# A four-layer graph network on one core: the last layer's unit loop written out, its destination keys copied by ScalarE, its sums spread over four PSUM banks

## The chip, the cores and the metric

The kernel runs on one core of a Trainium2 chip. The metric is the device time of one execution in microseconds (us). Before the change the median of three runs is 14387.95 us (14383.14 to 14405.51).

## The reference, cut to what matters

There are 12500 nodes with 64 features each and 400000 edges, sorted by destination. Four layers follow one another; each normalises x, clips it at zero and adds a graph operation to x. The change lies in the last layer:

```
message   = h[dst] * edge_weight[:, None]
neigh_agg = segment_sum(message, src, num_segments=12500)
x = x + (h @ W_self.T + b_self + neigh_agg @ W_neigh.T + b_neigh)
```

The edges are sorted by `dst`, but this layer sums over `src`, so its messages have to be brought into another order first.

## The kernel before, in words

A node is numbered by its lane (one of 128 partitions, called q here) and its place in the lane (one of 98, r). The last layer works in two parts.

The first part (`body4`, 125 blocks of 25 edges per lane) makes a record of 98 words for each edge: three bf16 planes of the message, whose sum is the fp32 message, and in the last two words the q of the node it belongs to. GpSimd scatters the records by indirect DMA (L1180) into `records` in DRAM, so that all records of one r lie together in groups of 512 (`SG`). There is room for 880 groups (`GMAX`).

The second part, which the change touches, walks over the 880 groups in 220 units (`UNITS`) of 4 groups (`UG`), 16 columns (`UC`) of 128 records each. For unit u:

- SyncE waits until unit u-4 has been summed (semaphore `unit_summed`), then loads the unit's 2048 records (784 KB) into one of four buffers `rows4[u % 4]` (L1095; semaphore `rows_in0` to `rows_in3`).
- VectorE copies each record's q twice into `qtwice[u % 2]` (bf16, L1671), and compares it with an iota row: this gives 16 one-hot matrices of 128 x 128 in `ohs4[u % 2]` (helper `row_onehots`, whose instruction is on L686; semaphore `unit_onehot`). It first waits for `unit_summed` of unit u-2, which frees that buffer.
- TensorE multiplies one-hots and message planes: 16 columns x 3 planes = 48 matmuls with 64 moving columns (L1971) into one PSUM bank, `bk[u % 2]`, 64 columns of the bank for each group. Before that it waits for `unit_running` of unit u-2, which frees the bank.
- VectorE adds the groups up in a chain (`unit_running`): running sum = previous running sum * mask + sum of this group, four instructions (L1684). The mask (`keepg`, one column per group) is zero where a new r begins. The four masks of a unit are first copied to `keep4` (L1675), as the column's number is in a register.
- ScalarE waits for `unit_running` and stores the four running sums (128 KB) to `by_lane`, a view of the DRAM tensor `sums` (L1825; semaphores `running_out0`, `running_out1`). The two `running` buffers alternate.

VectorE's order of work is written out: one-hots of u, running sums of u-1, one-hots of u+1, and so on. The helper `units` (L968) makes units 0 to 3 with numbers known at compile time, and the rest in a hardware loop of four units a turn, where waits compare with registers. `wait` issues a wait; `gate` issues a semaphore increment between two waits. `loop_chain` gives each VectorE instruction an increment of `v_loop` and a wait for it right behind; `clear` resets it.

When all 220 units are stored, the rows that end each r are fetched from `by_lane` (`fetch` on SyncE and ScalarE, L1188 on GpSimd), and the last matrix product and the output follow.

Of the kernel before, what the change touches and what calls it, by code (L numbers as in the profile page):

```python
# [14 lines left out]
N, E, D = 12500, 400000, 64  # L15
P = 128
# [5 lines left out]
BLOCKS = LANE // K  # L22
# [24 lines left out]
UG = 4  # L47
UNITS = GMAX // UG
RW = 98
# [8 lines left out]
def build(nc, x, src, dst, edge_weight, l0_w1, l0_b1, l0_w2, l0_b2, l1_w, l1_b,  # L58
          l2_w1, l2_b1, l2_w2, l2_b2, l3_ws, l3_bs, l3_wn, l3_bn, out):
    f32, bf16, i32, u8 = mybir.dt.float32, mybir.dt.bfloat16, mybir.dt.int32, mybir.dt.uint8  # L60
    ALU, ACT, AX = mybir.AluOpType, mybir.ActivationFunctionType, mybir.AxisListType
# [4 lines left out]
    with ctx:  # L66
        def sb(name, shape, dt=f32):
            return ctx.enter_context(nc.sbuf_tensor(name, shape, dt))

        def ps(name, shape):  # L70
            return ctx.enter_context(nc.psum_tensor(name, shape, f32))
# [3 lines left out]
        def sem(name):  # L75

            if name not in sems:
                sems[name] = ctx.enter_context(nc.semaphore(name))
            return sems[name]
# [23 lines left out]
        by_lane = sums.rearrange("(p g) f -> p g f", p=P)  # L103
# [20 lines left out]
        mblk = sb("mblk", [P, 2, K])  # L124
        rtwice = sb("rtwice", [P, K, 2], bf16)
        inrank, atbase = sb("inrank", [P, K]), sb("atbase", [P, K])
        keep4 = sb("keep4", [P, UG])
        ident_b = sb("ident_b", [P, P], bf16)
        laneg_i = sb("laneg_i", [P, 1], i32)
        endg_i = sb("endg_i", [P, TILES], i32)  # L130
# [55 lines left out]
        zero_row = sb("zero_row", [P, D])  # L186
# [13 lines left out]
        om = [ps(f"om{k}", [P, 512]) for k in range(2)]  # L200
# [5 lines left out]
        bk = [ps(f"bk{k}", [P, 512]) for k in range(2)]  # L206
# [9 lines left out]
        def mm_banks(name, u):  # L216
# [50 lines left out]
        keepg = flat(crow[:, :, :])[:, 0:GMAX]  # L267
        UC = UG * SUB_ROWS
        rows4 = [RF[:, k * UC * RW:(k + 1) * UC * RW].rearrange("p (c f) -> p c f", f=RW) for k in range(4)]
        planes4 = [[RF[:, k * UC * RW:(k + 1) * UC * RW].bitcast(bf16).rearrange("p (c f) -> p c f", f=2 * RW)  # L270
                    [:, :, a * D:(a + 1) * D] for a in range(3)] for k in range(4)]
        ohs4 = [RF[:, 4 * UC * RW + k * UC * P // 2:4 * UC * RW + (k + 1) * UC * P // 2].bitcast(bf16)
                .rearrange("p (c q) -> p c q", q=P) for k in range(2)]
        qtwice = [sb(f"qtwice{k}", [P, UC, 2], bf16) for k in range(2)]
        run_at = 4 * UC * RW + UC * P
        running = [RF[:, run_at + k * UG * D:run_at + (k + 1) * UG * D].rearrange("p (g f) -> p g f", f=D)
                   for k in range(2)]
# [19 lines left out]
        def wait(e, name, n):  # L297

            if not (isinstance(n, int) and n <= 0):
                e.wait_ge(sem(name), n)  # L300

        def gate(e):

            e.sem_inc(sem("gate_" + e.engine.name), 1)  # L304
# [378 lines left out]
        def row_onehots(e, to, twice, m):  # L683

            n = twice.shape[1]
            return e.tensor_tensor(to[:, 0:n, :].rearrange("p k (q h) -> p k q h", h=2),  # L686
                                   iota_b[:, 0:m].rearrange("p (q h) -> p q h", h=2).unsqueeze(1)
                                   .broadcast_to([P, n, m // 2, 2]),
                                   twice.unsqueeze(2).broadcast_to([P, n, m // 2, 2]), ALU.is_equal)
# [263 lines left out]
        NF = len(FILLQ)  # L953
        fill_banks = (tp[0], tp[1], om[0])
        msg_banks = (om[1], bk[0], bk[1], mixed)
        assert K == 8 * len(fill_banks) + 1


        def fetch(e, mine):

            e.wait_ge(sem("cleared"), 2)
            for k in range(2):
                e.wait_ge(sem(f"running_out{k}"), 16 * UNITS // 2 + 16 * (1 - k))
            for t in mine:
                g = e.value_load(endg_i[0:1, t:t + 1], min_val=0, max_val=GMAX)  # L965
                e.dma_start(M[:, t:t + 1, :], by_lane[:, bass.ds(g, 1), :]).then_inc(sem(f"rows_in{t // (4 * NT)}"), 16)  # L966

        def units(e, body):  # L968

            for k in range(4):  # L970
                body(k, k)
            with e.Fori(1, UNITS // 4) as j:  # L972
                for k in range(4):
                    body(j * 4 + k, k)
# [219 lines left out]
        def _(e):  # L1194
# [22 lines left out]
            def take_ab(p, t, n):  # L1217
# [7 lines left out]
                                         in1=dst_f[:, 0:LANE - 1], op0=ALU.add, op1=ALU.is_lt,  # L1225
# [6 lines left out]
            with unsorted(e):  # L1232
# [3 lines left out]
            loop_chain = Chain(e, "v_loop")  # L1236
# [9 lines left out]
                                         op0=ALU.add, op1=ALU.add))  # L1246
# [42 lines left out]
            for ins in divide_steps(e, src_v, LANE, src_q, src_r, src_i, src_i.bitcast(i32)):  # L1289
                chain(ins)  # L1290
            chain(e.scalar_tensor_tensor(out=src_v, in0=dst_f[:, :], scalar=float(P), in1=src_q,
                                         op0=ALU.mult, op1=ALU.add))
# [370 lines left out]
            e.sem_inc(sem("cleared"), 1)  # L1663


            def unit_onehots(u, k):
                wait(e, f"rows_in{k}", (u - k) * 4 + 16)
                gate(e)
                wait(e, "unit_summed", u - 1)
                gate(e)  # L1670
                loop_chain(e.tensor_copy(qtwice[k % 2][:, :, :], rows4[k][:, :, RW - 2:RW - 1].broadcast_to([P, UC, 2])))  # L1671
                row_onehots(e, ohs4[k % 2], qtwice[k % 2][:, :, :], P).then_inc(sem("unit_onehot"), 1)

            def unit_running(u, k):
                loop_chain(e.tensor_copy(keep4[:, :], keepg[:, bass.ds(u * UG, UG)]))  # L1675
                wait(e, "unit_summed", u + 1)
                gate(e)
                wait(e, f"running_out{k % 2}", (u - k % 2) * 8 + 16 * (1 - k % 2))
                gate(e)
                for g in range(UG):  # L1680
                    prev = running[k % 2][:, g - 1, :] if g else running[1 - k % 2][:, UG - 1, :]
                    if isinstance(u, int) and u + g == 0:
                        prev = zero_row[:, :]
                    loop_chain(e.scalar_tensor_tensor(out=running[k % 2][:, g, :], in0=prev, scalar=keep4[:, g:g + 1],  # L1684
                                                      in1=bk[k % 2][:, g * D:(g + 1) * D], op0=ALU.mult, op1=ALU.add))
                loop_chain.clear()
                e.sem_inc(sem("unit_running"), 1)

            def unit(u, k):
                unit_onehots(u, k)  # L1690
                if not (isinstance(u, int) and u == 0):
                    unit_running(u - 1, (k - 1) % 4)
            units(e, unit)
            unit_running(UNITS - 1, 3)
            for g in range(NGROUPS + 1):
                if g < NGROUPS:
                    mine = len([t for t in range(g // 2 * 2 * NT, (g // 2 + 1) * 2 * NT) if t % 3 == 0])
# [10 lines left out]
        def _(e):  # L1708
# [110 lines left out]
                            .then_inc(sem("middles"), 1)  # L1819
            loop(e, body4)  # L1820

            def unit(u, k):
                wait(e, "unit_running", u + 1)
                gate(e)
                e.dma_start(by_lane[:, bass.ds(u * UG, UG), :], running[k % 2])\  # L1825
                    .then_inc(sem(f"running_out{k % 2}"), 16)
            units(e, unit)
            fetch(e, range(2, TILES, 3))
            for g in range(NGROUPS):
                mm_scalar(e, "last", g)  # L1830
# [3 lines left out]
        def _(e):  # L1834
            e.wait_ge(sem("const"), 1)
            e.wait_ge(sem("checked"), 1)
            for c in range(2):
                last = e.matmul(pb[0:1, 0:1], bad[:, c:c + 1], ones[:, 0:1], start=c == 0, stop=c == 1)
# [9 lines left out]
            for g in range(NGROUPS // 2):  # L1848
                e.wait_ge(sem("rows_vector"), g + 1)
                for k in range(2 * NT):  # L1850
                    last = e.matmul(pa[:, :], mark_u[:, k // 2, :, k % 2], mark_v[:, k // 2, :, k % 2], start=g + k == 0,
                                    stop=g == NGROUPS // 2 - 1 and k == 2 * NT - 1, skip_group_check=True)
# [82 lines left out]
            for a in range(2):  # L1935
                last = e.transpose(pa[:, a * D:(a + 1) * D], w_lastT[:, a, :], ident[0:D, 0:D])
# [26 lines left out]
            def unit(u, k):  # L1963
                wait(e, "unit_onehot", u + 1)
                gate(e)
                wait(e, "unit_running", u - 1)
                gate(e)
                for c in range(UC):
                    g, part = c // SUB_ROWS, c % SUB_ROWS
                    for a in range(3):  # L1970
                        last = e.matmul(bk[k % 2][:, g * D:(g + 1) * D], ohs4[k % 2][:, c, :], planes4[k][a][:, c, :],  # L1971
                                        start=part + a == 0, stop=part == SUB_ROWS - 1 and a == 2)
                last.then_inc(sem("unit_summed"), 1)
            units(e, unit)
            mm_tensor(e, "last", D, "aggregated", 3 * NGROUPS)

# [22 lines left out]
```

## Time and profile before

| | us |
|---|---|
| median of 3 runs | 14387.95 |
| lowest, highest | 14383.14, 14405.51 |
| profiled execution, time | 14387.05 |
| profiled execution, span | 14385.3 |
| VectorE busy | 9170.4 (64% of the span) |
| GpSimd busy | 7813.4 (54%) |
| TensorE matmul busy | 7309.5 (51%) |
| ScalarE busy | 5834.6 (41%) |
| DMA, mean over the span | 137 GB/s |

The span is the time from the first to the last instruction in the trace. Busy times are sums over stages with different limits, so the rows read below are those of the second part of the last layer, from 13450 us to 14264 us of the span. The page calls the engines PE (TensorE), DVE (VectorE), ACT (ScalarE), POOL (GpSimd) and SP (SyncE); a q behind the name means the engine's sequencer or its DMA queue. The granted clock of TensorE is given as a share of its full speed: 1.00 is 2.4 GHz, 0.50 is 1.2 GHz.

### The profile page before, as it was taken

Reading aid. Unit: us, or ns where it says so; the run is one execution under the profiler, and the core shown is the slowest. Engines: PE = TensorE matmul, PEld = TensorE weight load, DVE = VectorE, ACT = ScalarE, POOL = GpSimd, SP = SyncE. Lnnn points to the kernel's source line nnn. Section 1 sums busy time; section 2 is a strip of 40 time slices with the busy share of each in tenths; the row PEclk is TensorE's granted clock in tenths of the full one; section 3 lists DMA queues with packets and bytes.
Section 4 is the critical chain, followed back from the end, with each engine's and each line's share of the span. In section 5 each row is a group of like instructions: output and inputs, shape, how many; then the busy total and the mean of one; then the engine's idle time right before and its main releaser. Section 6 shows DMA issues by size and latency. Waiting matters only on the chain. (4 is left out here: it accounts for less than half of the span.)

```text
span 14385.3 us, 285255 instructions
## 1 busy us (share of the span) xinstructions
PE 7309.5 (51%) x96792; PEld 5290.3 (37%) x96792; DVE 9170.4 (64%) x18447; ACT 5834.6 (41%) x10200; POOL 7813.4 (54%) x7194
## 2 busy tenths in 40 slices
PE   2266666666666646996999799600000000000355
PEld 1255555555555533553555555400000000000355
DVE  5488888888888884335333333466666666666575
ACT  0144444444444434774677477432222222222000
POOL 5677777777777751110111011377777777777300
PEclk9866666666666668997999899755555555555676
DMA  7333333333333328664866766322222222221585
GB/s 313 125 115 115 113 117 110 116 111 118 109 118 109 118 86 287 196 196 161 270 197 186 268 195 196 117 67 65 67 62 65 65 64 65 64 65 60 170 255 181
DMA packets 1267102, 1969.49 MB, mean 137 GB/s; under 512 B 255577, under 2 KB 986558, under 8 KB 1261425
## 3 DMA queue, kind: packets, MB, share of 16 engines
q1 hardware_dynamic: 861601, 1047.59, 24.0%
q10 hardware_dynamic: 172928, 612.08, 10.8%
q0 software_dynamic: 231664, 297.80, 7.7%
q8 instruction: 558, 9.14, 0.3%
q14 instruction: 351, 2.88, 0.1%
HBM read 1155.02 MB, written 815.55 MB: 137 GB/s over the span
## 5 line engine op out<-in xcount | busy, mean ns | idle before, releaser
L633 POOL DMA_INDIRECT RF<-tab_edge_b,idx x3125 | 3549.9, 1136 | 1029.5 <-issue 947.5
L1180 POOL DMA_INDIRECT records<-RF,idx x3125 | 3141.8, 1005 | 984.5 <-issue 984.5
L686 DVE TENSOR_TENSOR HM<-iota_b,eqw 128x2048 bf16<-128x2048 bf16 x2000 | 2204.3, 1102 | 344.8 <-PE bk L1865 198.0
L1739 ACT ACTIVATE X<-bk 128x392 uint8<-128x392 f32 x4000 | 1783.3, 495 | 1564.3 <-PE bk L1865 1546.1
L877 POOL DMA_INDIRECT agg<-RF,lastT x372 | 520.6, 1399 | 3209.9 <-ACT RF L819 3119.1
L1865 PE MATMUL bk<-HM 128*64 128x98 bf16 x32000 | 1581.3, 247 | 1310.0 <-ACT X L1739 661.2
L1865 PE MATMUL kp<-HM,ident_b 128*64 128x98 bf16 x6250 | 281.5, 283 | 3793.5 <-DVEq L1642 3793.5
L777 PE MATMUL tp<-HM,RF 128*64 128x512 bf16 x12276 | 2117.6, 383 | 91.0 <-ACT HM L729 66.3
L1865 PEld LDWEIGHTS bk<-HM 128*64 128x64 bf16 x32000 | 1237.2, 134 | 1657.4 <-issue 1575.6
L1865 PEld LDWEIGHTS kp<-HM,ident_b 128*64 128x64 bf16 x6250 | 261.5, 168 | 3814.5 <-issue 3814.5
L783 PE MATMUL om<-HM,RF 128*64 128x512 bf16 x6138 | 1422.2, 382 | 0.0
L777 PE MATMUL tp<-RF 128*64 128x512 bf16 x5952 | 1099.3, 388 | 262.8 <-ACT RF L729 236.9
L777 PEld LDWEIGHTS tp<-HM,RF 128*64 128x64 bf16 x12276 | 923.6, 110 | 727.7 <-issue 178.9
L1393 DVE SCALAR_TENSOR_TENSOR RF<-RF,dupjunk 128x64 f32<-128x64 f32 x3124 | 870.4, 279 | 27.3
L1393 DVE SCALAR_TENSOR_TENSOR RF<-RF,dupjunk,om 128x64 f32<-128x64 f32 x3124 | 848.5, 272 | 0.4
L1804 ACT ACTIVATE RF<-qblk 128x50 f32<-128x50 f32 x125 | 31.7, 254 | 1993.6 <-DMA records<-RF,idx 1940.7
L729 ACT ACTIVATE RF<-dst_f 128x4096 bf16<-128x4096 uint8 x186 | 672.8, 3617 | 354.7 <-PE tp L777 235.2
L729 ACT ACTIVATE HM<-dst_f 128x4096 bf16<-128x4096 uint8 (+1 forms) x186 | 703.5, 3823 | 138.2 <-DMA dst_f<-counts 89.9
L731 DVE CAST HM<-dst_f 128x4096 bf16<-128x4096 uint8 x186 | 426.9, 2295 | 500.9 <-PE tp L777 204.3
L783 PE MATMUL om<-RF 128*64 128x512 bf16 x2976 | 742.0, 388 | 0.0
L729 ACT ACTIVATE HM<-crow 128x4096 bf16<-128x4096 uint8 x186 | 671.6, 3611 | 54.2 <-DMA crow<-counts 40.6
L777 PEld LDWEIGHTS tp<-RF 128*64 128x64 bf16 x5952 | 496.2, 112 | 535.4 <-issue 299.4
(364 smaller groups left out, 15242.4 us busy)
## 6 DMA issues: line engine op xcount, KB each, us to landing
dst_f<-counts SPq DMA_DIRECT2D x465, 512.0 KB, 3.8
RF<-first_rows SPq DMA_DIRECT2D x250, 800.0 KB
counts<-X ACTq DMA_DIRECT2D x250, 784.0 KB
RF<-records SPq DMA_DIRECT2D x220, 784.0 KB
crow<-counts SPq DMA_DIRECT2D x279, 512.0 KB, 3.8
records<-RF ACTq DMA_DIRECT2D x2, 57680.0 KB, 214.4
first_rows<-RF ACTq DMA_DIRECT2D x25, 4000.0 KB, 49.4
edge_rows<-RF ACTq DMA_DIRECT2D x125, 800.0 KB
```

The costliest lines, as they stand in the source:

```text
L633: e.indirect_dma_start(out=ring[:, r, j, :], out_offset=None, in_=table[:, :], in_offset=bass.IndirectOffsetOnAxis(ap=idx[:, r, j:j + 1], ...
L686: return e.tensor_tensor(to[:, 0:n, :].rearrange("p k (q h) -> p k q h", h=2), iota_b[:, 0:m].rearrange("p (q h) -> p q h", h=2).unsqueeze ...
L729: e.activation(to, of, ACT.Copy).then_inc(sem("widened_A"), 1)
L731: e.tensor_copy(to, of).then_inc(sem("widened_D"), 1)
L777: last = e.matmul(tp[u][k * D:(k + 1) * D, :], hi_mid[:, t, k * D:(k + 1) * D], part, start=t == 0, stop=t == TILES - 1, skip_group_check= ...
L783: return e.matmul(om[u][k * D:(k + 1) * D, :], low[:, t, :], part, start=t < 2, stop=t >= TILES - 2, skip_group_check=True)
L877: e.indirect_dma_start(out=agg[:, :], out_offset=bass.IndirectOffsetOnAxis(ap=lastT[:, g * GB + k:g * GB + k + 1], axis=0), in_=out_rows[g ...
L1180: e.indirect_dma_start(out=records[:, :], out_offset=bass.IndirectOffsetOnAxis(ap=idx2[:, r, j:j + 1], axis=0), in_=msgs[MSG_OF[r]][:, j, ...
L1393: e.scalar_tensor_tensor(out=buf[:, r, j, :], in0=prev, scalar=mask[:, j:j + 1], in1=this, op0=op0, op1=op1).then_inc(sem(chain.name), 1)
L1739: e.activation(staged[u].rearrange("p (r k) -> p r k", k=P)[:, :, k:k + 4], bk[s % 2][:, 0:4 * TILES].rearrange("p (k r) -> p r k", k=4), ...
L1804: e.activation(msgs[MSG_OF[r]][:, :, RW - 2:RW], qblk[:, r, :].unsqueeze(2).broadcast_to([P, K, 2]), ACT.Copy)
L1865: last = e.matmul(to[k:k + D, :], by_q[:, k:k + D], by_r, start=start, stop=stop, skip_group_check=True)
```

## The change

ScalarE makes the copies of q, two units ahead of the stores (`unit_keys`), and signals them with `keyed`, a semaphore that stands at 125 (`BLOCKS`) by then. VectorE reads the masks in `keepg` directly, and its part and ScalarE's are unrolled in Python for all 220 units with constant numbers, with plain waits and no gates. The sums go to four PSUM banks in turn (`unit_banks`), and TensorE waits for `unit_running` of unit u-4 instead of u-2. SyncE and TensorE stay in the hardware loop.

```diff
--- before.py
+++ after.py
@@ -124,7 +124,6 @@
         mblk = sb("mblk", [P, 2, K])
         rtwice = sb("rtwice", [P, K, 2], bf16)
         inrank, atbase = sb("inrank", [P, K]), sb("atbase", [P, K])
-        keep4 = sb("keep4", [P, UG])
         ident_b = sb("ident_b", [P, P], bf16)
         laneg_i = sb("laneg_i", [P, 1], i32)
         endg_i = sb("endg_i", [P, TILES], i32)
@@ -953,6 +952,7 @@
         NF = len(FILLQ)
         fill_banks = (tp[0], tp[1], om[0])
         msg_banks = (om[1], bk[0], bk[1], mixed)
+        unit_banks = (bk[0], bk[1], om[0], om[1])
         assert K == 8 * len(fill_banks) + 1
 
 
@@ -1663,35 +1663,29 @@
             e.sem_inc(sem("cleared"), 1)
 
 
-            def unit_onehots(u, k):
-                wait(e, f"rows_in{k}", (u - k) * 4 + 16)
-                gate(e)
+            def unit_onehots(u):
+                e.wait_ge(sem("keyed"), BLOCKS + u + 1)
                 wait(e, "unit_summed", u - 1)
-                gate(e)
-                loop_chain(e.tensor_copy(qtwice[k % 2][:, :, :], rows4[k][:, :, RW - 2:RW - 1].broadcast_to([P, UC, 2])))
-                row_onehots(e, ohs4[k % 2], qtwice[k % 2][:, :, :], P).then_inc(sem("unit_onehot"), 1)
-
-            def unit_running(u, k):
-                loop_chain(e.tensor_copy(keep4[:, :], keepg[:, bass.ds(u * UG, UG)]))
-                wait(e, "unit_summed", u + 1)
-                gate(e)
-                wait(e, f"running_out{k % 2}", (u - k % 2) * 8 + 16 * (1 - k % 2))
-                gate(e)
+                row_onehots(e, ohs4[u % 2], qtwice[u % 2][:, :, :], P).then_inc(sem("unit_onehot"), 1)
+
+            def unit_running(u):
+                e.wait_ge(sem("unit_summed"), u + 1)
+                wait(e, f"running_out{u % 2}", (u - u % 2) * 8 + 16 * (1 - u % 2))
                 for g in range(UG):
-                    prev = running[k % 2][:, g - 1, :] if g else running[1 - k % 2][:, UG - 1, :]
-                    if isinstance(u, int) and u + g == 0:
-                        prev = zero_row[:, :]
-                    loop_chain(e.scalar_tensor_tensor(out=running[k % 2][:, g, :], in0=prev, scalar=keep4[:, g:g + 1],
-                                                      in1=bk[k % 2][:, g * D:(g + 1) * D], op0=ALU.mult, op1=ALU.add))
-                loop_chain.clear()
-                e.sem_inc(sem("unit_running"), 1)
-
-            def unit(u, k):
-                unit_onehots(u, k)
-                if not (isinstance(u, int) and u == 0):
-                    unit_running(u - 1, (k - 1) % 4)
-            units(e, unit)
-            unit_running(UNITS - 1, 3)
+                    prev = running[u % 2][:, g - 1, :] if g else running[1 - u % 2][:, UG - 1, :] if u else zero_row[:, :]
+                    if g:
+                        e.wait_ge(sem("v_loop"), u * (UG - 1) + g)
+                    else:
+                        wait(e, "unit_running", u)
+                    e.scalar_tensor_tensor(out=running[u % 2][:, g, :], in0=prev, scalar=keepg[:, u * UG + g:u * UG + g + 1],
+                                           in1=unit_banks[u % 4][:, g * D:(g + 1) * D], op0=ALU.mult, op1=ALU.add)\
+                        .then_inc(sem("v_loop" if g < UG - 1 else "unit_running"), 1)
+
+            for u in range(UNITS + 1):
+                if u < UNITS:
+                    unit_onehots(u)
+                if u:
+                    unit_running(u - 1)
             for g in range(NGROUPS + 1):
                 if g < NGROUPS:
                     mine = len([t for t in range(g // 2 * 2 * NT, (g // 2 + 1) * 2 * NT) if t % 3 == 0])
@@ -1819,12 +1813,21 @@
                             .then_inc(sem("middles"), 1)
             loop(e, body4)
 
-            def unit(u, k):
-                wait(e, "unit_running", u + 1)
-                gate(e)
-                e.dma_start(by_lane[:, bass.ds(u * UG, UG), :], running[k % 2])\
-                    .then_inc(sem(f"running_out{k % 2}"), 16)
-            units(e, unit)
+
+            def unit_keys(u):
+                k = u % 4
+                e.wait_ge(sem(f"rows_in{k}"), u // 4 * 16 + 16)
+                wait(e, "unit_onehot", u - 1)
+                e.activation(qtwice[u % 2][:, :, :], rows4[k][:, :, RW - 2:RW - 1].broadcast_to([P, UC, 2]), ACT.Copy)\
+                    .then_inc(sem("keyed"), 1)
+
+            unit_keys(0)
+            unit_keys(1)
+            for u in range(UNITS):
+                if u + 2 < UNITS:
+                    unit_keys(u + 2)
+                e.wait_ge(sem("unit_running"), u + 1)
+                e.dma_start(by_lane[:, u * UG:(u + 1) * UG, :], running[u % 2]).then_inc(sem(f"running_out{u % 2}"), 16)
             fetch(e, range(2, TILES, 3))
             for g in range(NGROUPS):
                 mm_scalar(e, "last", g)
@@ -1963,12 +1966,12 @@
             def unit(u, k):
                 wait(e, "unit_onehot", u + 1)
                 gate(e)
-                wait(e, "unit_running", u - 1)
+                wait(e, "unit_running", u - 3)
                 gate(e)
                 for c in range(UC):
                     g, part = c // SUB_ROWS, c % SUB_ROWS
                     for a in range(3):
-                        last = e.matmul(bk[k % 2][:, g * D:(g + 1) * D], ohs4[k % 2][:, c, :], planes4[k][a][:, c, :],
+                        last = e.matmul(unit_banks[k][:, g * D:(g + 1) * D], ohs4[k % 2][:, c, :], planes4[k][a][:, c, :],
                                         start=part + a == 0, stop=part == SUB_ROWS - 1 and a == 2)
                 last.then_inc(sem("unit_summed"), 1)
             units(e, unit)
```

## Rows read from the trace of the kernel before

**Rows 1.** The page's 40 slices: busy tenths of VectorE, granted clock tenths.
```profile
DVE  5488888888888884335333333466666666666575
...
PEclk9866666666666668997999899755555555555676
```

**Rows 2.** The page's chain that ended last, by line.
```profile
POOL records L1180 22%; DVE RF L1684 1%; PE bk L1971 1%; DVE RF L686 1%; PE om L383 0%; DVE qtwice L1671 0%; DVE keep L1675 0%; PE tp L370 0%; DVEq L304 0%; ACTq L965 0%; DVEq L300 0%; ACTq L966 0%; PE bk L370 0%; POOL first_rows L920 0%; DVEq L972 0%
```

**Rows 3.** A window of 250 us: us, busy time (instructions) by engine, clock, DMA.
```profile
13700.00:13950.00 250.00, 140.28 (x3279) 132.62 (x3275) 177.83 (x478) 0.00 (x0) 0.00 (x0) 0.78 0.81 255
```

**Rows 4.** Timeline over some units: start, us, instruction [idle before, releaser].
```profile
13702.33 1.59 PE L1971 MATMUL bk<-RF 128*128 128x64 bf16 x48 [1.90 <-DVE RF L686]
...
13704.63 0.18 DVE L1671 CAST qtwice<-RF 128x32 bf16<-128x32 f32 x1 [0.85 <-PE bk L1971]
13704.84 1.23 DVE L686 TENSOR_TENSOR RF<-iota_b,qtwice 128x2048 bf16<-128x2048 bf16 x1
13705.99 0.16 DVE L1675 COPY keep<-crow 128x4 f32 x1
...
13706.53 1.23 DVE L1684 SCALAR_TENSOR_TENSOR RF<-RF,keep,bk 128x64 f32<-128x64 f32 x4 [0.38 <-DVE keep L1675]
13708.16 0.18 DVE L1671 CAST qtwice<-RF 128x32 bf16<-128x32 f32 x1 [0.40 <-DVE RF L1684]
...
13709.90 2.72 PE L1971 MATMUL bk<-RF 128*128 128x64 bf16 x48 [1.58 <-DVE RF L686]
...
13719.29 0.18 DVE L1671 CAST qtwice<-RF 128x32 bf16<-128x32 f32 x1 [0.85 <-DVE RF L1684]
```

**Rows 5.** Groups by line and shape, 13500 to 14250 us: busy, mean, idle.
```profile
L1971 PE MATMUL bk<-RF 128*128 128x64 bf16 x9826 | 418.5, 212 | 333.0 <-DVE RF L686 333.0
...
L686 DVE TENSOR_TENSOR RF<-iota_b,qtwice 128x2048 bf16<-128x2048 bf16 x205 | 251.3, 1226 | 7.1
L1684 DVE SCALAR_TENSOR_TENSOR RF<-RF,keep,bk 128x64 f32<-128x64 f32 x819 | 230.0, 281 | 103.7 <-DVE keep L1675 81.8
L1671 DVE CAST qtwice<-RF 128x32 bf16<-128x32 f32 x204 | 37.0, 182 | 105.0 <-PE bk L1971 60.1 <-DVE RF L1684 44.9
L1675 DVE COPY keep<-crow 128x4 f32 x205 | 33.5, 163 | 0.0
```

**Rows 6.** Timeline of the first units of the second part.
```profile
13451.47 23.71 SPq L1095 DMA_DIRECT2D RF<-records  x9
13456.14 0.18 DVE L1671 CAST qtwice<-RF 128x32 bf16<-128x32 f32 x1 [84.67 <-DMA RF<-records]
...
13457.88 4.75 PE L1971 MATMUL bk<-RF 128*128 128x64 bf16 x96 [91.35 <-DVE RF L686]
```

**Rows 7.** One window while the first four loads land.
```profile
13454.00:13461.00 7.00, 3.12 (x59) 3.15 (x60) 3.04 (x6) 0.00 (x0) 0.00 (x0) 0.50 1.06 390
```

**Rows 8.** DMA queues, 13500 to 14250 us: packets, MB, share.
```profile
q1 hardware_dynamic: 108119, 164.43, 70.3%
q10 hardware_dynamic: 29436, 26.80, 11.1%
```

**Rows 9.** The store's line L1825 in the whole trace: durations ns, and landing.
```profile
L1825 ACTq DMA_DIRECT2D sums<-RF x220: 338/344/410, 13462.3 to 14264.1; - x110
...
DMA to landing us min/median/max: 1.7/2.1/4.8
```

**Rows 10.** Windows of 10 us with the two clock levels.
```profile
13520.00:13530.00 10.00, 7.43 (x134) 7.01 (x131) 7.17 (x19) 0.00 (x0) 0.00 (x0) 0.50 0.87 274
13540.00:13550.00 10.00, 4.59 (x143) 4.43 (x144) 7.11 (x20) 0.00 (x0) 0.00 (x0) 1.00 0.83 249
```

**Rows 11.** ScalarE's copy of q in the first part, L1804.
```profile
L1804 ACT ACTIVATE RF<-qblk x125: 248/250/273, 9332.0 to 13354.8; 128x50 f32<-128x50 f32 x125
```

**Rows 12.** Timeline behind the last unit: what GpSimd waited for.
```profile
14266.63 0.98 POOL L1188 DMA_INDIRECT HM<-sums,end_i  x1 [816.62 <-DMA sums<-RF]
```

**Rows 13.** The page's DMA queues: the instruction packets.
```profile
q8 instruction: 558, 9.14, 0.3%
```


## The prediction

> **What bounds the kernel now.** I read the page's slices first. The second part of the last layer lies in slices 38 and 39 of them, and VectorE is only 6 or 7 tenths busy there, while TensorE's granted clock is about 7 tenths [rows 1]; no engine is full on the face of it. The page's chain of what ended last then says where the part sits: behind GpSimd's scatter (L1180) with 22% come the part's own lines, L1684, L1971, L686, L1671 and L1675 [rows 2]. So the part is on the path. It begins at 13456 us with the first copy of q [rows 6], and GpSimd's fetch at 14266.63 us, which waited 816.62 us for stores to `sums`, shows that nothing behind it starts before the last store [rows 12]. A microsecond won in a unit is won 220 times.
>
> A window in its middle gives VectorE 177.83 us of 250 us, DMA a share of 0.81 at 255 GB/s and matmuls 140.28 us [rows 3]. The timeline shows what the 250 us are made of. The reader is to compare the copy of q at 13704.63 us with the one at 13719.29 us: both have the long gap of 0.85 us ahead of them, that of the loop's turn, and they are four units apart, so a unit takes 14.66 / 4 = 3.66 us [rows 4]. The groups agree: 205 units in 750 us, 3.66 us each [rows 5]. Within a unit VectorE goes without a break except for waits of its own making: copy of q 0.18, one-hots 1.23, mask copy 0.16, a gap of 0.38, four sums 1.23, a gap of 0.40 [rows 4]. The gaps stay as long when the matmuls last 1.59 us as when they last 2.72 us, and TensorE idles 333.0 us in 750 us waiting for one-hots (L686) [rows 4, 5]. VectorE with its semaphore steps is the bound, not TensorE and not the loads: 220 x 3.66 = 805 us.
>
> **The change part by part.**
>
> *VectorE.* Gone are the copy of q (37.0 us / 204 = 0.18 us), the mask copy (33.5 / 205 = 0.16 us, of which 0.08 us lies over the end of the one-hots, 13704.84 + 1.23 - 13705.99) [rows 4, 5], the gates, the clear with its increment, and the loop's turn, 0.85 - 0.40 = 0.45 us in four units or 0.11 us a unit [rows 4]. What stays is 1.23 + 1.23 = 2.46 us, the latter with the waits between the sums in it: 4 x 0.281 is 1.12, so a satisfied wait on the engine's own last result costs (1.23 - 1.12) / 3 = 0.035 us [rows 4, 5]. Left between them are three waits ahead of the sums and two ahead of the one-hots. From below they cost nothing (they pass while the engine still works, as the mask copy began before the one-hots ended); from above, the gap of 0.40 us holds six semaphore steps, 0.07 us each, so five cost 0.35 us [rows 4]. I take 0.14, nearer to the wait of 0.035 us, since the reset and the increments that drained the engine are gone. VectorE then needs 2.60 us a unit, bounds 2.46 and 2.81. The masks read in place cost nothing: a scalar operand of the same kind, another address.
>
> *What is late next.* Four candidates stand close together.
>
> Loads and stores: a unit moves 784 KB in and 128 KB out, 0.934 MB. While the first four loads landed, the queues moved 390 GB/s [rows 7]; at that rate a unit takes 2.39 us, the lower bound. In the steady state the share was 0.81 of 3.66 us, which is 2.97 us if a packet takes as long when the queues are full [rows 3]; that is the upper bound. The queues' rows say the same: 70.3% + 11.1% of 750 us over 204 units is 2.99 us [rows 8]. The share in the first window is 1.06 at 390 GB/s, so packets get faster when the queue is full (368 GB/s at a share of one, against 255 / 0.81 = 315); I take 2.65 us, nearer to that window. The Trainium skill ("DMA: Bandwidth & Descriptors", Where 436 GB/s comes from) puts HBM's limit for one core at about 358 GB/s; by it a unit would be 0.934 / 358 = 2.61 us, an estimate. This trace shows more for these very loads, 390 GB/s, so the row goes before the page here.
>
> Matmuls: 1.59 us at the full clock and 2.72 us at half [rows 4, 10]. With two one-hot buffers a unit's ring over two periods is: sums 1.23, one-hots 1.23, TensorE's start behind them (copy of q at 13708.16, 0.21 us to the one-hots as in the unit before, 1.23 us of them, so 13709.60; matmuls at 13709.90: 0.30 us), matmuls, and an assumed 0.1 us back to VectorE. At half clock 1.23 + 1.23 + 0.30 + 2.72 + 0.1 = 5.58, or 2.79 us a unit; with the waits I take 2.85. At full clock it is 4.45 / 2 = 2.22 us, no bound. The two units in the first rows run 96 matmuls in 4.75 us without a break, so TensorE's own loop adds nothing that I can see [rows 6]. The four banks take the wait for the sums of u-2 away; the one-hot buffers still tie unit u to the matmuls of u-2, so the banks alone buy little, and I give them 0 (they cannot cost either: same matmuls, other addresses).
>
> ScalarE: a copy of q, 0.25 us for a similar one [rows 11], and the store's issue of 0.34 us [rows 9], 0.6 us of 2.7. It has been idle here but for the issues. What queues behind its waits: the store of u stands behind the copy of q for u+2, and that behind `rows_in` of u+2; the copy for u+3 stands behind the store of u, hence behind the sums of u. VectorE wants that copy only after one-hots u+2 and sums u+1, 2.5 us later, which covers 0.34 + 0.25 and the semaphores. At the stage's start the detour costs about 0.3 us once.
>
> Stores: `running[u % 2]` is free when the store of u has landed. Two periods must hold sums 1.23, ScalarE's hop 0.2, landing 2.1 (median) to 4.8 (longest) [rows 9]: 3.5 to 6.2 us, so 1.8 to 3.1 us a unit. The median is no bound. Loads: the first copy of q came 4.67 us behind the first load's issue [rows 6]; a load is issued when u-4 is summed, some 2.5 periods before it is wanted, so it has 6.5 us.
>
> *Sum.* At full clock max(2.60, 2.65, 2.22) = 2.65 us, at half clock 2.85 us. The clock was 0.78 in the middle, which is 0.56 of the time at 1.00 and 0.44 at 0.50, as the windows show it flip between the two [rows 3, 10]. I keep that mix: 0.56 x 2.65 + 0.44 x 2.85 = 2.74 us. 220 x 2.74 = 603 us against 805, 202 us less. The profiled execution took 14387.05 us, 0.9 us less than the median of the runs, so the sum may be taken from the median: 14388 - 202 = 14186 us. Bounds of the unit, 2.50 to 3.10 us, give 14133 to 14265 us.
>
> **Rivals.**
>
> *The transfers bound at their steady price.* If a packet keeps its length of the steady state, a unit needs 2.97 us: 14388 - 220 x 0.69 = 14236 us. For it: the share of 0.81 is that of many packets, the 390 GB/s of a few; stores lie between the loads there. Against: the share of 1.06 at a higher rate.
>
> *The clock stays up.* Matmuls would fill 1.59 of 2.6 us instead of 1.59 of 3.66, and the gaps between bursts shrink from 2.1 to 1.0 us. If TensorE is then granted 1.00 throughout and waits hide under work, a unit takes 2.50 us: 14388 - 255 = 14133 us. For it: it was 1.00 in stretches with matmuls busy only 4.6 of 10 us, and their share will rise [rows 10]. Against: it was 0.50 in stretches with matmuls busy 7.4 of 10 us [rows 10]. The Trainium skill ("TensorE: Matmul & The Clock Gate", HAM oscillation) says likewise that idle gaps throw the clock back and short ones keep it; the trace shows the flip itself, not what gap it takes.
>
> *The store waits in ScalarE's queue.* Stores behind `rows_in` of u+2 land late and each takes the longest landing, 4.8 us [rows 9], plus 0.3 for the copy: 2T = 1.23 + 0.2 + 0.34 + 0.3 + 4.8, T = 3.4 us, and 14331 us. For it: stores share the engines with loads that are now back to back. Against: a median of 2.1 us at a share of 0.81.
>
> *Slower: code that starves.* VectorE and ScalarE now run straight through code for 220 units instead of turning in a loop, and that code comes by DMA, past queues that the loads fill: the page has 558 instruction packets of 9.14 MB in all, 16.4 KB each [rows 13]. If an engine stood still for a late packet for the longest landing seen, 4.8 us [rows 9], the 202 us won are gone after 42 such stops; at one stop in every four units, 55 of them, it is 14186 + 264 = 14450 us. Against: the packets took 0.3% of the engines over the whole span, and five or ten instructions a unit is little code. The Trainium skill ("Runtime: NRT & Kernel Launch", Instruction fetch mechanics) says that a block holds 256 instructions and is fetched ahead, and that straight code hides it; by it some 2600 instructions on VectorE are 10 blocks, 48 us by the price above if none were hidden, an estimate.
>
> *It does nothing,* because something the trace doesn't name sets 3.66 us: 14388 us. The gaps' regularity speaks against it.
>
> **How the numbers follow.** The forecast 0.50 (its own range 14150 to 14225), transfers 0.22, clock up 0.13, stores late 0.08, starving code 0.05, nothing 0.02. Within 0.2% (29 us) is about what a measurement of this kernel can't tell from no change. Faster is 0.50 + 0.22 + 0.13 + 0.08 = 0.93, same 0.02, slower 0.05. The range of 8 in 10 takes in the first three cases: 14115 (2.42 us a unit, the transfers' lower bound rounded) to 14275 us (3.15).
>
> **What would show it.** Copies of q and L1675 gone from VectorE, and a period of 2.6 to 2.9 us; one-hots that begin right behind the sums, or 0.1 us later. If the waits ahead of the one-hots end with `keyed` and the DMA share is near 1, the transfers bound; if the sums wait for L1971 in stretches of clock 0.50 only, the matmuls' ring does; if they wait for nothing but stores have landings over 4 us, the `running` buffers do. The time from the last store to the end should stay about 121 us. The forecast is wrong if the period is above 3.1 us, or if VectorE shows stops that no semaphore explains.

## The result and the profile after

The changed kernel took 14163.34 us (median of 4 executions, 14156.65 to 14175.62) against 14385.55 us for the kernel before (14375.16 to 14405.51, 4 executions): ratio 0.9846, 95% interval 0.9832 to 0.986, so 222 us or 1.5% faster. The forecast was 14186 us, 202 us faster.

The page of the changed kernel answers to [rows 1]: VectorE's tenths and the granted clock.

```profile
DVE  5388888888888885335333433366656666656585
...
PEclk9866666666666667998999799955555555555598
```

The last two clock digits were 7 and 6 and are 9 and 8. The windows of the second part, 250 us and 500 us long, answer to [rows 3] (us, busy time and instructions of PE, PEld, DVE, ACT, POOL, clock, DMA share, GB/s):

```profile
13700.00:13950.00 250.00, 155.66 (x4530) 146.78 (x4531) 211.19 (x472) 21.84 (x94) 0.00 (x0) 0.97 1.02 353
13500.00:14000.00 500.00, 308.27 (x8896) 290.71 (x8892) 416.00 (x928) 43.22 (x186) 0.00 (x0) 0.97 1.01 347
```

VectorE went from 177.83 to 211.19 us busy in 250 us, the DMA share from 0.81 to 1.02, the clock from 0.78 to 0.97. How long the part takes is read from what GpSimd's first fetch waited for, as in [rows 12], where it was 816.62 us:

```profile
14055.10 0.98 POOL L1188 DMA_INDIRECT HM<-sums,end_i  x1 [609.33 <-DMA sums<-RF]
```

816.6 - 609.3 = 207.3 us are the part's own. The profiled spans differ by 14385.3 - 14173.9 = 211.4 us; the rest lies ahead of the part, whose first load is issued 4.2 us earlier, at 13447.24 instead of 13451.47 us. From the fetch to the end it is 118.7 us before and 118.8 us after. A unit takes 609.3 / 220 = 2.77 us if the start and the end of the part are shared out over the units, and 500 / 186 = 2.69 us in its middle, by the groups that answer to [rows 5]:

```profile
L685 DVE TENSOR_TENSOR RF<-iota_b,qtwice 128x2048 bf16<-128x2048 bf16 x186 | 226.6, 1218 | 0.3
...
L1680 DVE SCALAR_TENSOR_TENSOR RF<-RF,crow,bk 128x64 f32<-128x64 f32 x372 | 104.3, 280 | 39.5 <-DMA sums<-RF 27.0 <-PE bk L1974 0.7 <-issue 0.4
L1680 DVE SCALAR_TENSOR_TENSOR RF<-RF,crow,om 128x64 f32<-128x64 f32 x370 | 103.7, 280 | 44.2 <-DMA sums<-RF 33.1
L1821 ACT ACTIVATE qtwice<-RF 128x32 bf16<-128x32 f32 x186 | 43.2, 232 | 457.3 <-DMA RF<-records 378.2 <-DVE RF L1680 66.2 <-DVE RF L685 12.9
```

Both copies are gone from VectorE, and nothing is idle ahead of the one-hots (0.3 us in 500). Ahead of the sums 39.5 + 44.2 = 83.7 us are idle, and 27.0 + 33.1 = 60.1 us of them are put down to the store, `DMA sums<-RF`; for most of the rest the view names nothing. The timeline, to be read beside [rows 4], shows both kinds of unit:

```profile
13708.28 1.23 DVE L1680 SCALAR_TENSOR_TENSOR RF<-RF,crow,bk 128x64 f32<-128x64 f32 x4
...
13709.42 1.22 DVE L685 TENSOR_TENSOR RF<-iota_b,qtwice 128x2048 bf16<-128x2048 bf16 x1
13709.54 0.34 ACTq L1830 DMA_DIRECT2D sums<-RF  x1
...
13710.66 1.23 DVE L1680 SCALAR_TENSOR_TENSOR RF<-RF,crow,bk 128x64 f32<-128x64 f32 x4
...
13711.06 1.60 PE L1974 MATMUL om<-RF 128*128 128x64 bf16 x48 [0.79 <-DVE RF L685]
...
13711.92 0.34 ACTq L1830 DMA_DIRECT2D sums<-RF  x1
...
13715.84 0.23 ACT L1821 ACTIVATE qtwice<-RF 128x32 bf16<-128x32 f32 x1 [3.07 <-DMA RF<-records]
13716.27 1.23 DVE L1680 SCALAR_TENSOR_TENSOR RF<-RF,crow,om 128x64 f32<-128x64 f32 x4 [0.93 <-DMA sums<-RF]
13717.42 1.22 DVE L685 TENSOR_TENSOR RF<-iota_b,qtwice 128x2048 bf16<-128x2048 bf16 x1
```

From the sums at 13708.28 to those at 13710.66 us is 2.38 us: sums and one-hots follow each other with no gap to speak of. The one-hots start 0.09 us ahead of the end of the sums, the sums 0.02 us behind the end of the one-hots. The sums at 13716.27 us waited 0.93 us for a store. Their buffer's earlier store had been issued at 13711.92 us; they start 4.35 us later. Stores now land later than in [rows 9] (2.1 us median, 4.8 at most):

```profile
DMA to landing us min/median/max: 1.7/3.8/6.1
```

The timelines also show what a store lands with. SyncE issues the load of unit u+2 once TensorE is through with u-2, a little ahead of the store of u-2. Here is that load for the store at 13711.92 us, and the landing of all loads:

```profile
13710.54 0.37 SPq L1095 DMA_DIRECT2D RF<-records  x1
```

```profile
DMA to landing us min/median/max: 4.3/5.3/9.1
```

The load had landed when ScalarE's copy of q, which waited for it, started at 13715.84 us, 5.30 us after its issue; the store, issued 1.38 us behind it, landed by 13716.27 us, 0.43 us behind the load. In 126 of the 217 units behind the first three the sums start 0.4 us after such a copy. In run4 below, where the sums wait for no store, none do. So the store's landing seems to be set by the load issued just ahead of it. That is read from the timelines; no run changed the order of the two, so it isn't shown.

### The profile page after: what moved, and what is told of

It reads as the page before. It is cut to its first block and busy times, and to the rows that moved or that the text cites. A ratio compares the mean times of both kernels' runs of the same rounds, so it can differ in the third digit from the quotient of the medians.

```text
span 14173.9 us, 282965 instructions
## 1 busy us (share of the span) xinstructions
PE 7230.5 (51%) x96792; PEld 5213.9 (37%) x96792; DVE 9087.6 (64%) x18007; ACT 5880.2 (41%) x10420; POOL 7807.9 (55%) x7194
```

## The experiments

The part's length is GpSimd's wait for `DMA sums<-RF`; divided by 220 it is the length of a unit with the part's start and end in it. It is taken from one profiled execution of each kernel. Kernels with the same time of the kernel before beside them ran together, on one chip.

| kernel | time, us (median) | before beside it | part, us | per unit, us |
|---|---|---|---|---|
| before | 14385.55 | | 816.6 | 3.71 |
| changed | 14163.34 | 14385.55 | 609.3 | 2.77 |
| run4 | 14121.49 | 14383.55 | 554.4 | 2.52 |
| half_loads | 14080.76 | 14383.55 | 514.8 | 2.34 |
| banks_only | 14382.86 | 14383.55 | 815.8 | 3.71 |
| two_banks | 14143.63 | 14383.55 | 577.6 | 2.63 |
| after_again | 14173.28 | 14381.69 | 609.0 | 2.77 |
| unrolled_only | 14181.9 | 14381.69 | 612.8 | 2.79 |
| written_out | 14152.92 | 14381.69 | 596.0 | 2.71 |
| run4_two_banks | 14115.21 | 14381.69 | 553.4 | 2.52 |
| after_third | 18822.64 | 19051.63 | 592.2 | 2.69 |
| two_banks_again | 18818.31 | 19051.63 | 592.0 | 2.69 |
| vector_keys | 18795.44 | 19051.63 | 575.2 | 2.61 |
| keys_run4 | 18794.6 | 19051.63 | 564.5 | 2.57 |

The last four ran together on a chip where the kernel before takes 19052 us instead of 14384; the second part of the last layer has about its usual length there, other stages don't. They are compared with one another only, and by the length of the part.

**run4: four buffers of running sums.**

```diff
-                   for k in range(2)]
+                   for k in range(4)]
...
+        out_sems = (("running_out0", 16), ("running_out1", 0), ("lane_placed", 32), ("records_zeroed", 48))
...
-                wait(e, f"running_out{u % 2}", (u - u % 2) * 8 + 16 * (1 - u % 2))
+                e.wait_ge(sem(out_sems[u % 4][0]), u // 4 * 16 + out_sems[u % 4][1])
...
-                    prev = running[u % 2][:, g - 1, :] if g else running[1 - u % 2][:, UG - 1, :] if u else zero_row[:, :]
+                    prev = running[u % 4][:, g - 1, :] if g else running[(u - 1) % 4][:, UG - 1, :] if u else zero_row[:, :]
```

(`running[u % 4]` in the sums and the store too, and the fetches wait for all four semaphores.)

> The changed kernel with four buffers for the running sums instead of two; everything else as changed. After the change a unit takes 2.69 us, VectorE's own work 2.37 us. Theory A, the ring of the two buffers for running sums: a store lands 3.7 us (median) behind its issue, and the sums of u+2 wait for it. With four buffers that wait goes, and a unit falls to 2.40 to 2.50 us: 45 to 60 us less than the changed kernel (14163), about 14110. Theory B, the transfers' rate: the queues are full (share 1.00 at 347 GB/s) and the late stores are only where that shows. The unit stays at 2.65 to 2.70 us, the time within 10 us of 14163, and the wait moves to the copy of q, so to the loads.

Measured: 14121.49 us (14112.16 to 14130.0), ratio to before 0.9819 (0.9803 to 0.9835). The end of the part, and VectorE's and ScalarE's longest waits in it (us in total, times, longest):

```profile
13995.87 0.98 POOL L1189 DMA_INDIRECT HM<-sums,end_i  x1 [554.43 <-DMA sums<-RF]
```

```profile
DVE RF L685 <- ACT qtwice L1822: 27.1, 64, 1.3
DVE RF L1681 <- PE bk L1975: 1.1, 2, 0.9
```

```profile
ACT qtwice L1822 <- DMA RF<-records: 476.4, 213, 3.5
```

VectorE no longer waits for a store, though stores land later still:

```profile
DMA to landing us min/median/max: 1.7/4.7/6.2
```

Theory A holds: the two `running` buffers were the changed kernel's bound. The time is 42 us less than the changed kernel's, where 45 to 60 were forecast. In the window below VectorE runs 510 instructions, five a unit, so 102 units; a unit takes 250 / 102 = 2.45 us, where the changed kernel has 2.69, and that is inside the 2.40 to 2.50 forecast. The next bound stands right behind it: 27.1 us now go to one-hots that wait for copies of q, and 213 of the 220 copies wait for their load.

```profile
13500.00:13750.00 250.00, 162.53 (x4895) 153.07 (x4896) 225.81 (x510) 23.72 (x102) 0.00 (x0) 1.00 1.05 381
```

The queues run at 381 GB/s. That is the 0.934 MB of a unit over its 2.45 us, so it is no second proof; what speaks for the loads as the bound here are the waits. So Theory B named the second limit, not the first.

**half_loads: half of each load.** The kernel leaves out two of the four groups of records in every load; all other work stays.

```diff
-                e.dma_start(rows4[k].rearrange("p (g c) f -> p g (c f)", c=SUB_ROWS),
+                e.dma_start(rows4[k].rearrange("p (g c) f -> p g (c f)", c=SUB_ROWS)[:, 0:2, :],
...
-                            .rearrange("(g p c) f -> p g (c f)", g=UG, p=P)).then_inc(sem(f"rows_in{k}"), 16)
+                            .rearrange("(g p c) f -> p g (c f)", g=UG, p=P)[:, 0:2, :]).then_inc(sem(f"rows_in{k}"), 16)
```

> The changed kernel, but each load brings only two of the unit's four groups of records; the other half of the buffer keeps what it held, so the sums of those groups are left wrong. 0.52 MB move per unit instead of 0.93. Theory B (transfers' rate): a unit falls to VectorE's own 2.37 us plus little, 2.40, and the time to about 14100; stores land after 2.1 us again. Theory A (the ring of buffers, a fixed landing): also faster only if landings shorten, so landings stay near 3.7 and the unit near 2.65. A third theory, TensorE's clock: with fewer waits the clock stays at 1.00; if it fell to the mix of before, units in stretches of clock 0.50 would take 2.85 and the mean 2.6.

Measured: 14080.76 us (14073.82 to 14091.76), 19 us below the forecast. The window and the landing of its stores:

```profile
13500.00:13750.00 250.00, 174.76 (x5261) 164.52 (x5262) 237.83 (x550) 25.36 (x109) 0.00 (x0) 1.00 0.76 233
```

```profile
DMA to landing us min/median/max: 1.7/2.4/4.4
```

With two buffers as in the changed kernel the unit falls to 2.34 us, or 250 / 110 = 2.27 us in this window. VectorE is busy for 237.83 of 250 us: this is its floor. Stores land after 2.4 us instead of 3.8. So the ring of two buffers binds only because full queues lengthen the landing: both theories name a half of it. The clock is 1.00 in this window.

**banks_only: the four banks put into the kernel before.**

```diff
+        unit_banks = (bk[0], bk[1], om[0], om[1])
...
-                                                      in1=bk[k % 2][:, g * D:(g + 1) * D], op0=ALU.mult, op1=ALU.add))
+                                                      in1=unit_banks[k][:, g * D:(g + 1) * D], op0=ALU.mult, op1=ALU.add))
...
-                wait(e, "unit_running", u - 1)
+                wait(e, "unit_running", u - 3)
...
-                        last = e.matmul(bk[k % 2][:, g * D:(g + 1) * D], ohs4[k % 2][:, c, :], planes4[k][a][:, c, :],
+                        last = e.matmul(unit_banks[k][:, g * D:(g + 1) * D], ohs4[k % 2][:, c, :], planes4[k][a][:, c, :],
```

> The kernel before with the four banks of sums alone. My step: the banks buy nothing, as VectorE is the bound and the one-hot buffers tie unit u to u-2 anyway: 3.66 us a unit, within 10 us of the kernel before. Rival: the banks let TensorE start earlier and save 0.1 us a unit or more, 20 us or more.

Measured: 14382.86 us (10 executions, 14376.63 to 14392.96), ratio 1.0 (0.9991 to 1.001); the part 815.8 against 816.6 us. Nothing, as forecast.

**two_banks, after_again, after_third, two_banks_again: the changed kernel with two banks and with four.** The edit takes back the three places above (`unit_banks[u % 2]`, `unit_banks[k % 2]`, `u - 1`); after_again and after_third are the changed kernel unchanged.

> The changed kernel with two banks of sums instead of four. My step: the banks buy nothing, so 2.69 us a unit and within 10 us of the changed kernel. Rival: now that VectorE has no slack, TensorE has to wait for the sums of u-2, which end only when the one-hots of u begin; since these end later than the sums, still no wait. Only if sums come late behind stores does TensorE wait for them: then up to 0.1 us a unit, 20 us.

Measured: 14143.63 us (14133.34 to 14167.71), the part 577.6 us. That is 20 us less than the changed kernel's 14163, twice what was expected at most, but the two didn't run together.

> The changed kernel itself, beside its variants on one chip. The variant with two banks took 14144 us where the changed kernel had taken 14163, though the order of work cannot differ between them. Theory C: it is scatter between executions, since the stores' landing behind full queues varies; then this run is between 14135 and 14175 us and overlaps the two banks' 14133 to 14168. Theory D: four banks cost something by themselves; then it is again 14155 or more in each execution.

Measured: 14173.28 us (14170.58 to 14192.96), the part 609.0 us. By its own bounds this spoke for Theory D.

> The changed kernel once more, beside its variant with two banks, on one chip. Theory C (scatter between executions of stores that land late): the two medians lie within 10 us of each other, and their executions overlap. Theory D (four banks cost something while there are two buffers of running sums): this one is 15 to 30 us slower than the other, as 14170 stood to 14144 before.

> The changed kernel with two banks of sums, beside the changed kernel. Theory C: within 10 us of it. Theory D: 14145, 15 to 30 us faster than it.

Measured on one chip, 4 executions each: 18822.64 us (18808.23 to 18837.24) and 18818.31 us (18782.81 to 18827.33), the part 592.2 and 592.0 us. Here Theory C holds, the banks do nothing. The difference of 20 to 30 us in the earlier runs did not come back; the order of work is the same in both kernels, since VectorE makes the one-hots of u after the sums of u-2, and TensorE needs those one-hots: with two banks its wait for the sums of u-2 is always met by then. What differs in the profiles with 609 and with 578 us is how long the sums waited for stores, first the changed kernel and then two_banks, each 13450 to 14200 us:

```profile
DVE RF L1680 <- DMA sums<-RF: 76.1, 93, 2.6
```

```profile
DVE RF L1680 <- DMA sums<-RF: 44.6, 76, 1.9
```

76.1 - 44.6 = 31.5 us, the whole difference of the parts (609.3 - 577.6 = 31.7). Each is one execution, and the times of all executions overlap (14156.65 to 14175.62 and 14133.34 to 14167.71 us). Why stores were late more often in some sets of runs than in others is open, and so parts that didn't run together can't be told apart within some 30 us.

**unrolled_only and written_out: the writing out alone.** Both have two banks, no `unit_keys` on ScalarE, and VectorE copies q; unrolled_only copies the masks too.

```diff
-                e.wait_ge(sem("keyed"), BLOCKS + u + 1)
+                e.wait_ge(sem(f"rows_in{u % 4}"), u // 4 * 16 + 16)
                 wait(e, "unit_summed", u - 1)
+                e.tensor_copy(qtwice[u % 2][:, :, :], rows4[u % 4][:, :, RW - 2:RW - 1].broadcast_to([P, UC, 2]))\
+                    .then_inc(sem("keyed"), 1)
+                e.wait_ge(sem("keyed"), BLOCKS + u + 1)
...
+                wait(e, "unit_running", u)
+                e.tensor_copy(keep4[:, :], keepg[:, u * UG:(u + 1) * UG]).then_inc(sem("looked"), 1)
+                e.wait_ge(sem("looked"), BLOCKS + u + 1)
```

(The last three lines are in unrolled_only alone.)

> VectorE and ScalarE written out without gates, but VectorE still copies q and the four masks itself, and the sums use two banks. My step: VectorE's floor of 2.37 us plus 0.22 for the copy of q with its wait, 0.16 to 0.20 for the masks: 2.80 us a unit, 14385 - 220 x 0.86 = 14196 us. So nine tenths of the win would come from the writing out. Rival: the copies, not the gates, were the cost; then 3.3 us a unit, 14306 us.

Measured: 14181.9 us (14170.03 to 14183.22), 14 us below the forecast, the part 612.8 us:

```profile
14062.93 0.98 POOL L1189 DMA_INDIRECT HM<-sums,end_i  x1 [612.81 <-DMA sums<-RF]
```

With both copies kept, the writing out alone wins 816.6 - 612.8 = 203.8 us, where the whole change won 207.3, so more than the nine tenths expected. The run takes out the gates, the register waits, the clear and the loop's turns together; what each of them costs isn't shown. Its sums hardly wait for stores (8.3 us in the whole part):

```profile
DVE RF L1687 <- DMA sums<-RF: 8.3, 14, 1.4
```

> As the last, but the masks are read in place: VectorE still copies q, two banks. VectorE 2.37 + 0.22 = 2.60 us a unit. Theory A (two buffers of running sums bound at the landing of the stores): the changed kernel's VectorE waits 0.3 us a unit for stores, so this one hides the copy of q in that wait and takes 2.65 to 2.70 us, 14160 us, as the changed kernel: ScalarE's copies buy nothing. Rival: stores land later by as much as VectorE is later, and it takes 2.90 us, 14210 us.

Measured: 14152.92 us (14152.07 to 14164.27), the part 596.0 us (2.71). The forecast of Theory A holds: with the copy of q on VectorE it is not slower than the changed kernel, which took 14173.28 us beside it. The step from unrolled_only, 612.8 - 596.0 = 16.8 us or 0.08 us a unit, is what reading the masks in place gives.

**vector_keys and keys_run4: VectorE copies q, four banks, with two and with four buffers.** Edits as above.

> The changed kernel with four banks of sums, but VectorE copies q itself; the same with two banks took 14153 us. Theory C: 14153 within 10 us. Theory D: 14170 or more. Either way the sums wait less for stores than in the changed kernel, as VectorE has 0.2 us a unit more to do.

> Four buffers of running sums, four banks, but VectorE copies q itself. With ScalarE's copies the four buffers took 14121 us, 2.51 us a unit. With the ring of stores gone, ScalarE's copies should show their worth: VectorE needs 2.37 + 0.22 = 2.59 us a unit, so 2.60 and 14140 us, 20 us slower than with ScalarE's. Rival: the transfers bound alone, then 2.51 us and 14121.

Measured by the part: 575.2 and 564.5 us, 2.61 and 2.57 us a unit, where the changed kernel beside them had 592.2. The absolute times forecast don't apply there; 18795.44 and 18794.6 us against 18822.64 are 27 and 28 us less. For vector_keys 17 us of that lie in the part, and the rest doesn't. The sums of vector_keys waited little for stores, first vector_keys, then the changed kernel on the same chip:

```profile
DVE RF L1683 <- DMA sums<-RF: 7.3, 22, 0.6
```

```profile
DVE RF L1680 <- DMA sums<-RF: 57.8, 76, 2.6
```

So with two buffers ScalarE's copies of q did not help; here they cost 592.2 - 575.2 = 17 us of the part, as between after_again and written_out, 13 us. Why they cost, instead of doing nothing, is open. (two_banks, with ScalarE's copies, had 577.6 us and written_out 596.0, the other way round, but these two did not run together.) With four buffers the part is 564.5 us with VectorE's copies, and was 554.4 us with ScalarE's on another chip: 10 us, where 20 were forecast, and less than what parts of different chips can show.

**run4_two_banks.** Both edits together.

> The changed kernel with four buffers of running sums and two banks of sums. The four buffers alone gave 14121 us, 2.51 us a unit. Theory C (banks do nothing, scatter by stores): 14121 within 10 us. Theory D (four banks cost 20 us): 14100.

Measured: 14115.21 us (14114.29 to 14123.48), ratio to before 0.9817 (0.9801 to 0.9834); the part 553.4 us against run4's 554.4. Theory C again. It and run4 beat both kernels: 14163.34 - 14121.49 = 42 us and 48 us less than the changed kernel, and 14173.28 - 14115.21 = 58 us less than the changed kernel that ran beside it.

## Why the prediction was right, point by point

- *The bound before.* Right: VectorE with its semaphore steps. unrolled_only keeps every copy and takes out only gates, register waits, the clear and the loop's turns, and gains 204 us. One reading was off: a slice is 359.6 us, so the part lies in the last three slices, where VectorE is 5, 7 and 5 tenths busy [rows 1], not in two with 6 or 7. Nothing was worked out from it.
- *VectorE's new floor, 2.60 us.* Too high. The sum of its pieces ignored that one-hots and sums overlap: 2.38 us in the timeline, 2.27 us a unit in half_loads' window, both below the lower bound of 2.46. The satisfied waits cost nothing visible; the 0.14 us for five of them should have been below nothing.
- *Transfers, 2.65 us, bounds 2.39 and 2.97.* Too high too: in run4 a unit's transfers took 2.45 us, at 381 GB/s. The lower bound from the window of the first loads, 390 GB/s, was nearer, and the rival at 2.97 us is refuted: the same packets take less of the engines' time when the queues are full, 0.81 x 3.66 = 2.96 us a unit before and 1.05 x 2.45 = 2.57 us in run4. The Trainium skill's limit of about 358 GB/s for one core's HBM traffic ("DMA: Bandwidth & Descriptors", Where 436 GB/s comes from) is exceeded here, by 381 GB/s over 250 us.
- *The clock.* The term 0.44 x 2.85 for half clock is wrong: the granted clock was 0.97 in both windows, not 0.78, and in those of run4 and half_loads 1.00. TensorE's bursts still last 1.59 us; its gaps went from 1.90 us [rows 4] to 0.79 us where nothing is late. VectorE waited for matmuls 3.7 us in the whole part. The rival on the clock was right about the clock; its unit of 2.50 us is near what run4 shows (2.52), not what the changed kernel does (2.77).
- *The stores.* I took the median of 2.1 us and found no bound. It is 3.8 us now: 2T = 1.23 + 0.03 + 3.8 + 0.1 = 5.16 (the last term as assumed in the prediction), or 2.58 us a unit for the median landing. Early landings can't make up for late ones, up to 6.1 us, as VectorE has its own floor; that would explain the rest up to 2.69, but isn't shown. That is the bound of the changed kernel (run4), and the step of the sum that was mis-sized. The mechanism I named for a rival, stores held up behind ScalarE's copies, is not it: each store was issued 0.03 us behind its sums, 0.04 at most over 219 units of the timeline, as at 13711.92 us above.
- *The sum.* 2.74 us forecast, 2.69 to 2.77 measured. The number is right partly by luck, because terms that were too high (VectorE, transfers, clock) stood where the stores' term was missing.
- *Banks, 0.* Right (banks_only, after_third beside two_banks_again).
- *ScalarE's copies.* They were to take 0.18 us a unit off the bound. They did take it off VectorE, but the bound had moved to the stores, and the kernels with the copies on VectorE were 13 us (written_out, two banks) and 17 us (vector_keys) faster in the part. They added nothing to the win.
- *Starving code.* Of VectorE's stops in the part only 0.4 us have no store, matmul or load behind them; it did not happen.

## What to carry to other kernels

When an engine's own work is a chain of 0.2 to 1.2 us instructions, count the semaphore and loop steps between them: here they were 0.9 of 3.7 us a unit, and writing the loop out with constant numbers got nearly the whole gain. Once such a stage fills the DMA queues, read landings again at that load before sizing buffers; each buffer that waits for a store needs the landing under load, not the one seen at a share of 0.81. Look also at what is issued just ahead of the store. Work moved off an engine that then waits for transfers bought nothing here.

## What the runs showed of the hardware that was not expected

- Packets get faster as queues fill: 255 GB/s at a share of 0.81, 381 GB/s at 1.05 (run4), with the same mix of packets. That is 315 and 363 GB/s at a share of one.
- The store's landing, 128 KB: 2.1 us at 255 GB/s, 2.4 at 233 GB/s (half_loads), 3.8 at 347, 4.7 at 381 (run4). The rate alone doesn't set it: in keys_run4 it was 3.8 us at 373 GB/s, on another chip.
- The granted clock went from 0.78 to 0.97 when the gaps between the same bursts of 48 matmuls shrank.
- The same kernel took 14173 us (after_again) and 18823 us (after_third) on two chips, with this part about the same (609 and 592 us). TensorE's and GpSimd's busy tenths fell in the first stages; the cause is open.
